# Softmax attention on TensorE: one order inside every gap of the schedule, one pair's split moved behind the output product, and inverse sums that travel as rows

## What is computed

```
q, k = rope(x @ Wq), rope(x @ Wk);  v = x @ Wv          # 4 query heads share one key head
attn = softmax(q @ k.T * 64 ** -0.5, axis=-1)           # 512 x 512 for each head
out  = (attn @ v) @ Wo + bo
x    = layernorm(x + out)
```

## Time and profile before

| | |
|---|---|
| median of 3 runs | 3483.9 us (3481.72 to 3492.31) |
| profiled execution | 3476.33 us, of which the traced span is 3474.6 us |
| TensorE matmuls, over the span | 2916.5 us busy (84%) |
| VectorE, ScalarE, GpSimd | 2036.1, 1343.6, 963.2 us busy |
| mean granted TensorE clock | 0.914 of full speed |
| first score transposes and last store of this layer | 69.4 us and 1279.5 us into the span |

### The profile page before, as it was taken

The page is one execution under the profiler, slowest core; times in us unless marked ns, Lnnn a source line. Parts: engine busy times, 40 slices in busy tenths (PEclk is TensorE's granted clock), DMA queues, the critical chain, the costliest instruction groups (busy, mean ns, idle before and its releaser), DMA issues. The chain is left out here.

```text
span 3474.6 us, 61109 instructions
## 1 busy us (share of the span) xinstructions
PE 2916.5 (84%) x16442; PEld 2043.2 (59%) x16443; DVE 2036.1 (59%) x3929; ACT 1343.6 (39%) x2751; POOL 963.2 (28%) x1303
## 2 busy tenths in 40 slices
PE   6999898989989857877999999969888888837993
PEld 4565565656556536765777777744444445416992
DVE  3656565565656537764665656557566666635664
ACT  3545454544545422212222222215444444424443
POOL 3434342333424112113333333310111111121225
PEclk8999999999999978988999999979888898968996
DMA  2111111111111120120000000023211121124225
GB/s 66 32 26 37 34 28 31 29 38 25 37 28 28 28 72 31 36 100 19 13 12 12 12 12 12 7 65 78 61 50 53 54 55 54 43 67 158 73 73 189
DMA packets 190113, 163.02 MB, mean 47 GB/s; under 512 B 85754, under 2 KB 153490, under 8 KB 189330
## 3 DMA queue, kind: packets, MB, share of 16 engines
q1 hardware_dynamic: 178836, 138.40, 14.5%
q0 software_dynamic: 6912, 18.96, 1.4%
q10 hardware_dynamic: 4224, 4.19, 0.3%
HBM read 87.73 MB, written 37.06 MB: 36 GB/s over the span
## 5 line engine op out<-in xcount | busy, mean ns | idle before, releaser
L1120 ACT ACTIVATE soft_probs<-soft_ps_s,soft_mx 128x512 f32<-128x512 f32 x512 | 354.7, 693 | 413.1 <-DVE soft_mx L1042 400.7
L1042 DVE TENSOR_REDUCE soft_mx<-soft_ps_s 128x1 f32<-128x512 f32 x512 | 346.3, 682 | 247.0 <-PE soft_ps_s L952 205.8
L1844 DVE TENSOR_REDUCE mla_mx<-mla_ps_s 128x1 f32<-128x512 f32 x512 | 334.4, 685 | 240.4 <-PE mla_ps_s L1704 216.4
L1947 ACT ACTIVATE mla_pt<-mla_ps_t 128x512 f32<-128x512 f32 x512 | 292.0, 600 | 396.0 <-PE mla_ps_t L1716 356.7
L961 PE MATMUL soft_ps_p<-ident,soft_probs 128*128 128x128 f32 x2048 | 326.0, 283 | 68.7 <-ACT soft_probs L1120 45.6
L952 PE MATMUL soft_ps_s<-soft_ks,soft_qs 128*128 128x512 f32 x1024 | 373.9, 447 | 0.0
L961 PEld LDWEIGHTS soft_ps_p<-ident,soft_probs 128*128 128x128 f32 x2048 | 245.2, 144 | 189.8 <-DVE soft_mx L1042 98.5
L970 PE MATMUL soft_ps_a<-soft_pt,soft_v 128*64 128x512 f32 x1024 | 284.3, 635 | 24.1 <-DVE soft_ri L1046 15.6
L1052 DVE COPY soft_pt<-soft_ps_p 128x512 f32<-128x512 f32 x256 | 176.2, 688 | 137.3 <-PE soft_ps_p L961 135.4
L1704 PE MATMUL mla_ps_s<-mla_stack,mla_pad 128*128 128x512 f32 x512 | 234.7, 465 | 24.2 <-DVE mla_mx L1844 19.1
L1716 PE MATMUL mla_ps_t<-mla_shifted,mla_pad 128*128 128x512 f32 x512 | 223.8, 439 | 29.6 <-ACT mla_pt L1947 27.0
(11 more groups left out here) (334 smaller groups left out, 6609.2 us busy)
## 6 DMA issues: line engine op xcount, KB each, us to landing
soft_rrep<-inverse SPq DMA_DIRECT2D x128, 128.0 KB, 3.1
mla_pad<-mla_stack SPq DMA_DIRECT2D x256, 64.0 KB, 2.0
moe_xt<-by_expert SPq DMA_DIRECT2D x72, 129.0 KB, 2.0
soft_ks<-soft_ks SPq DMA_DIRECT2D x64, 128.0 KB, 2.4
raw<-in_L_ffn_w SPq DMA_DIRECT2D x16, 512.0 KB, 8.2
mla_stack<-mla_yh SPq DMA_DIRECT2D x128, 64.0 KB, 2.1
soft_xc<-in_L_attn_x SPq DMA_DIRECT2D x8, 512.0 KB, 4.7
soft_xb<-in_L_attn_x SPq DMA_DIRECT2D x8, 512.0 KB, 4.0
```

The source lines that it names most:

```text
L1042: op = vv.tensor_reduce(out=mx[:, h, t:t + 1], in_=ps_s[:, s_bank(4 * h + t), :], axis=AX.X, op=ALU.max, negate=True)
L1120: op = nc.scalar.activation(probs[:, h % 2, t, :], ps_s[:, s_bank(4 * h + t), :], ACT.Exp, bias=mx[:, h, t:t + 1], scale=1.0, accum_out=rs ...
L1844: op = vv.tensor_reduce(out=mx[:, a, t, s:s + 1], in_=ps_s[:, (16 * a + 4 * t + s) % S_BANKS, :], axis=AX.X, op=ALU.max, negate=True)
L1947: op = nc.scalar.activation(pt[:, t % 2, s, :], ps_t[:, s % 2, :], ACT.Exp, scale=KPH ** -0.5)
```

## The change

Four things change. In every gap the steps of TensorE are sorted by kind: P first, then RT, T, QT and KT, then A, then S, then Q, KV and W. On VectorE the maxima M go last in their gap. OH 0 and OL 0 move six gaps later, from gap 52 to 58. The inverse sums of a pair take another way to DRAM: TensorE transposes the 128 x 8 block to 8 x 128 (RT, in PSUM through the two `misc` banks), ScalarE copies it to `rrow` (RC), and RW writes eight rows of 512 bytes in place of 1024 single values; RW and RR are put one gap later. RT is a ninth kind of user of the two banks, so it also shifts which product uses which bank: W 3, for one, comes to share its bank with W 2, and QT 0 1 0 with Q 0 2.

```
--- before.py
+++ after.py
@@ -706,7 +706,7 @@
         pt = sb("pt", [P, RING, TT, SEQ])
         probs = sb("probs", [P, 2, TT, SEQ])
         rs, ri, mx = (sb(n, [P, HEADS, TT]) for n in ("rs", "ri", "mx"))
-        rrep = sb("rrep", [P, SEQ])
+        rrep, rrow = sb("rrep", [P, SEQ]), sb("rrow", [P, P])
         ot = sb("ot", [P, SEQ])
         ath, atl = (sb(n, [P, PAIRS, SEQ], F32R) for n in ("ath", "atl"))
         r = sb("r", [P, 2, D])
@@ -757,8 +757,8 @@
             for c in range(TT):
                 put(attend(p, c), "tensor", ("A", p, c))
             at = attend(p, TT - 1) + 1
-            put(at, "vector", ("O", p)); put(at, "gpsimd", ("OH", p), ("OL", p))
-            put(S0 + 8 * p + 10, "sync", ("RW", p), ("RR", p))
+            put(at, "vector", ("O", p)); put(at if p else at + 6, "gpsimd", ("OH", p), ("OL", p))
+            put(S0 + 8 * p + 10, "tensor", ("RT", p)); put(S0 + 8 * p + 10, "scalar", ("RC", p)); put(S0 + 8 * p + 11, "sync", ("RW", p), ("RR", p))
 
         def project(at, u):
             put(at, "tensor", u)
@@ -795,6 +795,10 @@
             put(S0 + g, "scalar", ("X", h, c))
 
         S, ahead, order = {}, {}, {}
+        turn = {"P": 0, "RT": 1, "T": 1, "QT": 1, "KT": 1, "A": 2, "S": 3, "Q": 4, "KV": 4, "W": 4, "M": 1}
+        for g in range(ROUND):
+            for eng in ENGINES[:2]:
+                gaps[g, eng] = sorted(gaps.get((g, eng), []), key=lambda k: turn.get(k[0], 0))
         for eng in ENGINES:
             order[eng] = [k for g in range(ROUND) for k in gaps.get((g, eng), [])]
             ahead[eng] = [k for k in order[eng] if k in ahead_keys[eng]]
@@ -804,7 +808,7 @@
         misc = [k[:2] if k[0] == "W" else k for k in order["tensor"] if k[0] not in ("S", "P", "A") and not (k[0] == "W" and k[2])]
         bank = {k: n % 2 for n, k in enumerate(misc)}
         emptied = {"T": lambda k: (dve_s, ("XL", k[1])), "KV": lambda k: (dve_s, ("VC", k[1])), "Q": lambda k: (dve_s, ("ROT",) + k),
-                   "QT": lambda k: (act_s, ("C",) + k), "KT": lambda k: (act_s, ("C",) + k), "W": lambda k: (dve_s, ("F", k[1]))}
+                   "RT": lambda k: (act_s, ("RC", k[1])), "QT": lambda k: (act_s, ("C",) + k), "KT": lambda k: (act_s, ("C",) + k), "W": lambda k: (dve_s, ("F", k[1]))}
         units = [k for k in order["tensor"] if k[0] in ("Q", "KV")]
         st_place = {("HI",) + k: n % 2 for n, k in enumerate(u for u in units if u[0] == "Q")}
         rt_place = {("ROT",) + k: 0 for k in units}
@@ -840,6 +844,7 @@
             def _(sp):
                 for s in range(2):
                     sp.sem_inc(stored[s], 32)
+                sp.sem_inc(inverse_out, 16)
                 (raw_q, _, _), (raw_kv, _, _), (raw_o, _, _) = raw_and_parts
                 own = owner("sync")
                 batch = lambda ap, index: ap[bass.ds(index, 1), :, :].rearrange("o (t p) d -> p (o t) d", p=P)
@@ -860,12 +865,12 @@
                             sp.dma_start(ks[to, 1, g, :].bitcast(F32), ks[at, 0, g, :].bitcast(F32)).then_inc(swapped[g], 16)
                     elif kind == "RW":
                         j, p = own(i, key), key[1]
-                        hold(sp, *dve_s.at(j, "I", 2 * p + 1))
+                        hold(sp, *act_s.at(j, "RC", p))
                         hold(sp, *(dve_s.at(j, "O", p - 1) if p else dve_s.at(shift(j, -1), "O", PAIRS - 1)))
-                        sp.dma_start(inverse.rearrange("s (t p) -> p s t", p=P), ri[:, 2 * p:2 * p + 2, :], allow_slow_non_contiguous=True).then_inc(inverse_out, 16)
+                        sp.dma_start(inverse.rearrange("s (t p) -> (s t) p", p=P), rrow[0:2 * TT, :]).then_inc(inverse_out, 16)
                     elif kind == "RR":
                         j, p = own(i, key), key[1]
-                        hold(sp, inverse_out, 128 * j[0] + (128 * j[1] + 16 * p + 16))
+                        hold(sp, inverse_out, 128 * j[0] + (128 * j[1] + 16 * p + 32))
                         for s in range(2):
                             sp.dma_start(rrep[HD * s:HD * s + HD, :], inverse[s].partition_broadcast(HD)).then_inc(inverse_in, 16)
                     elif kind == "ST":
@@ -933,6 +938,10 @@
                             for a in range(4):
                                 at = 2 * HD * (4 * b + a)
                                 last = nc.tensor.transpose(m[:, P * a:P * a + P], st[:, st_place[("HI",) + u], at:at + 2 * HD], ident[:, :])
+                        elif kind == "RT":
+                            p = key[1]
+                            pe.wait_ge(*dve_s.at(j, "I", 2 * p + 1))
+                            last = nc.tensor.transpose(m[0:2 * TT, 0:P], ri[:, 2 * p:2 * p + 2, :].rearrange("p s t -> p (s t)"), ident[:, :])
                         elif kind == "KT":
                             at = 2 * HD * key[1]
                             pe.wait_ge(*pool_s.at(j, "LO", "KV", TT - 1))
@@ -1110,6 +1119,11 @@
                                 g = k[1]
                                 act.wait_ge(*pe_s.at(shift(j, -1), "S", GRP * g + GRP - 1, 3))
                                 op = nc.scalar.copy(ks[:, 0, g, :], ps_m[:, bank[k], :])
+                        elif kind == "RC":
+                            p = key[1]
+                            act.wait_ge(*pe_s.at(j, "RT", p))
+                            act.wait_ge(inverse_out, 128 * j[0] + (128 * j[1] + 16 * p + 16))
+                            op = nc.scalar.copy(rrow[0:2 * TT, :], ps_m[0:2 * TT, bank["RT", p], 0:P])
                         elif kind == "X":
                             h, t = key[1:]
                             act.wait_ge(*dve_s.at(j, "M", h, t))
```

## The result

The changed kernel takes 3421.0 us (median of 4 runs, 3418.5 to 3423.3) beside 3482.8 us for the kernel before in the same session: a ratio of 0.983, 95% interval 0.981 to 0.984. It is faster by 1.7%, where 0.8% was forecast. The profiled execution has a span of 3416.7 us, 57.9 less than before; the working of the prediction gave 28.6.

The account below looks back on a forecast made before the run. TensorE was taken to set the pace, its idle time to count. Seven batches -14.4 us, first +1.5, last -15.7: -28.6, so 3476.3 becomes 3447.7 profiled; the median lies 7.6 higher, forecast 3455 us, range 3438 to 3472.

Parts of the forecast that it names:

- later split: Gaps 56 to 58: TensorE's 5.91 us wait and the half clock after it go; gain 8.3 us a batch.
- maxima last: VectorE: F, ROT and O no longer stand behind a maximum, so three TensorE waits go; gain 2.7 us a batch.
- later scores: Scores start later in their gap, so the next head's first P comes later; cost 3.9 us a batch in all.
- rotation of Q 0 0: Gap 15: the maximum M stands behind this rotation; cost 0.65 us a batch.
- QT 0 1 0 at its bank: Gap 22: QT 0 1 0, now early, waits for the rotation of Q 0 2; cost 0.75 us a batch.
- W 3 at its bank: W 3 waits for F 2, which stands behind E 3 2 in the same gap; cost 0.8 us a batch.
- P, A, S instead of P, S, A: TensorE's new order: +0.05 us in each of 23 gaps, about -0.05 in 9; cost 0.7 us a batch.
- the change leaves it alone: Turn of the loop: TensorE's 20.7 us of waits while ScalarE starts its next round were taken to stay.
- RW as rows: Write to read takes 2.4 us, at most 10.6; nothing in the loop waits long; gain 15.7 us once, last batch.
- The last batch: O 7 at 1243.5 instead of 1260.0 on the old time scale, W 3 losing 0.8; gain 15.7 us, once.
- rival (a): Costs of order and banks hide in each other and are half: 31 us less, 3424 us; chance 0.17.
- Rival (c): The path from scores to the next head's transposes becomes the pace: 56 us more, 3511 us; chance 0.1.

Follow-up runs that it names:

- e1: The kernel before with only OH and OL of the first pair moved later; ratio 0.990 to the kernel before.
- e5: As e1, with the store of token tile 1 put ahead of RW 1 and RR 1 in SyncE's gap 54; ratio 0.983 to the kernel before.
- e2: The kernel before with only the order within gaps changed, on both TensorE and VectorE; ratio 1.010 to the kernel before.
- e6: The changed kernel with VectorE alone sorted and TensorE in its old order; ratio 0.969 to the kernel before.
- e7: The changed kernel itself once more, on the chip of e5, e6 and e8; ratio 0.985 to the kernel before.
- e8: The changed kernel with neither engine sorted, so both in their old order; ratio 0.979 to the kernel before.
- e9: As e6, with F first in its gap and the rotation of Q 0 0 behind the maximum; 3308.2 us, ratio 0.960 to the kernel before.
- e10: As e8, with one more write of 1024 single values behind RR 2 in gap 63; ratio 0.980 to the kernel before.

## Why the prediction was off

The direction was right, and most terms of the rest held. The size was half of what was measured. By the prediction's own steps, for one batch, from the gaps of the profile before and after (means of seven; gaps 3 and 4, inside the turn, of six):

| step | forecast | measured |
|---|---|---|
| later split, gaps 56 to 58 (with QT 1 3 0 for F 3) | -7.9 | -7.6 |
| maxima last, gaps 14, 37, 53 | -2.7 | -2.8 |
| later scores, gaps 35 and 36 | +0.93 | +0.87 |
| later scores behind QT, gaps 20, 28, 44, 60 and the one before each | +1.4 | +1.05 |
| rotation of Q 0 0, gap 16 | +0.65 | +0.60 |
| QT 0 1 0 at its bank, gap 22, with an RT | +1.05 | +1.30 |
| W 3 at its bank, gap 55 | +0.8 | +0.9 |
| P, A, S instead of P, S, A, and the other six RT and RC | +2.5 | +1.4 |
| rest, gap 5 to 61 | -3.3 | -4.2 |
| later scores, gaps 3 and 4 | +0.93 | +0.77 |

**The steps that failed** are two. The first is on the turn of the loop: "the change leaves it alone". But the prediction books 1.2 us of cost inside each turn, for gaps 3, 4 and 62, 8.6 us in seven. These costs came (1.1 us a turn), but the seven turns together are 0.3 us shorter. Gaps 1 and 2 fell from 10.4 to 4.5 us, while gaps 63 and 0 rose from 3.9 to 8.4: the wait of 20.7 us for E that the sentence speaks of is gone, and one for X stands in its place. This step is off by 9 us, the largest part that belongs to the change.

The second is on RW as rows: "Inside the loop nothing waits for it long, and behind it in the queue only LB, ST and KD stand, which come sooner." That they come sooner was costed at nothing, and the later split was costed at 8.3 us without it. e1 shows that the split without it brings 34 us instead of 58, and e5, which changes only the place of one store in SyncE's queue, brings the rest. Nor does nothing wait for it: O 3 does, and by e2 the gain in gap 14 (0.8 us a batch) takes the rows as well as the maxima. This did not spoil the forecast of the sum, because the change has all parts; but it was right by luck, and the terms stood at the wrong parts.

**Where the 29 us lie** by which the profiled time is below the forecast:

- Seven rests, 6 us. P, A, S and six RT together cost 1.4 us a batch for 2.5. RT was too dear: the row has 0.27 us, and four gaps with an RT are 0.11 us longer than their like, two 0.25 to 0.28, for 0.3 each.
- Seven turns, 9 us, the step above.
- The last batch, 5 us: it gave 20.5 for 15.7. The chain up to RT 7 was right: on the old time scale it falls at 1235.8, for 1236. From RT 7 to O 7 it is 5.4 us for 7.5, since RW to RR is 1.27 for 2.4 and RT to RW 0.73 for 1.6. From O 7 to the last store it is 18.3 us, where it was 19.9 and 0.8 more was forecast.
- The start, -2 us: it cost 3.4 for 1.5. Of these, 2.2 lie ahead of the layer's first score transposes (71.6 us for 69.4) and are not explained.
- The other layers, 11 us, by the clock of that execution. That they came on the side of the gain is luck.

In the last batch TensorE is idle 15.2 us less and busy 5.3 us less. The whole end of the layer and the part behind O 7, before and after (after the busy times comes the clock):

```profile
1181.00:1279.90 98.90, 73.52 (x383) 46.03 (x381) 42.89 (x81) 33.31 (x83) 16.71 (x21) 0.87 0.11 26
1260.00:1279.90 19.90, 12.88 (x84) 12.50 (x84) 6.42 (x17) 0.00 (x0) 5.03 (x10) 0.76 0.06 21
```

```profile
1154.70:1233.10 78.40, 68.24 (x387) 42.10 (x387) 41.06 (x80) 34.70 (x88) 14.35 (x20) 1.00 0.07 23
1214.80:1233.10 18.30, 12.09 (x95) 11.30 (x94) 6.41 (x17) 0.00 (x0) 5.02 (x10) 1.00 0.07 22
```

With the long waits (13.3 and 8.0 us) the clock is 0.87 over the whole and 0.76 in the last part; without them it is 1.00.

Against rival (a), costs that hide in each other, stands the table: most of the costs are there. Its time was closest by accident. Rival (c), the path from scores to the next transposes, was not decisive in the change. It is one part of what TensorE's order costs, by e6 and e7 53 us, of which seven rests are 38. Of the 5.5 us of a rest, the path has 1.9 (gap 36, and those behind QT), the banks of QT 0 1 0 and QT 1 3 0 1.8, gap 14 0.5. The prediction's terms for these gaps (0.7 for the order, 2.3 of the path, 1.15 for the banks of QT) make 4.2.

What stays open: why the turn of the loop is 17.7 us with rows and 20.2 with columns (e8, e5). The column write in flight explains 1.0 at most. What the gaps show is where the time goes. With columns, gaps 1 and 2 are 2.79 and 5.44 us long (e5), with rows 1.01 and 3.50 (e8), and gap 2 is often at a lower clock: 0.53 to 0.70 in all six turns of the first profile of before, 1.00 in all six after. One of them, before and after:

```profile
1029.33:1034.91 5.58, 5.23 (x17) 2.68 (x18) 4.82 (x9) 1.04 (x3) 0.00 (x0) 0.69 0.52 142
```

```profile
1006.34:1009.81 3.47, 3.47 (x17) 2.12 (x16) 2.03 (x5) 2.48 (x6) 1.56 (x1) 1.00 0.00 0
```

What makes TensorE late in these gaps, the earlier load of the residual or the engines' own restart, nothing here separates.

## What to carry to other kernels

- When a long stall is to go, ask of every queue what was hidden behind that stall, SyncE's above all. A store behind a read that waits for a slow write cost some 24 of 58 us here.
- An order that is good for one engine is not good for the other. Maxima last on VectorE gained 31 us; the sort of TensorE, with scores late, lost 53. Scores begin the longest chain (S, M, X, P: 2.4 us), and this chain has 1.9 of the 5.5 us that a rest lost; the banks have as much. Sort the consumers for whoever waits, and try the producer of the longest chain first. One kernel shows this, so it is a thing to try and not a rule.
- With buffers handed out in turn, one more step shifts all that follow it. Check who is the new partner of each, and place the release first in its gap: the two moves of e9 were worth 1.6 us a batch.

## What was not expected of the hardware

- A write of 1024 single values makes the whole loop unsteady, not only slow. The seven rests vary from 131.2 to 132.8 and 132.1 to 135.8 us in the two profiles of before and from 125.9 to 129.8 in e1. With rows they agree within 0.05 us in every profile (127.79 to 127.83, 122.32 to 122.35, 120.71 to 120.76), and with e10's one column write they spread again (126.7 to 128.3).
- That write delays a transfer behind it in the same queue that it has nothing to do with: in e10 the load of the residual lands 13.0 us after its issue for 4.7 in e8, and the longest wait for it grew from 8.7 to 18.1 us. (The Trainium skill, "DMA: Bandwidth & Descriptors", section "Queues, rings and completion order", says that each DMA engine takes the descriptors of one queue in order; the delay agrees with that.)
- The same code runs at another clock in another session. From its first matmul to that of the fifth layer, the fourth takes 782.7 us in the profile of before and 782.2 in that of after, at a granted clock of 0.87, and 735.6 to 743.2 us in the ten of the experiments, on three chips, at 0.90 to 0.92. TensorE is busy 648 us in the first two and 612 to 624 in the others. Whether chip or hour makes the difference is not shown. Ratios between sessions carry such a part.
